# Two 16-head attentions and a rank-32 feed-forward in an eight-stage kernel: banks paired, set-up moved inside, small matmuls tiled

## What is computed

```python
# x: (32, 256, 128), 16 heads of 8 columns
x = x + _L0_attn_ref(_layernorm(x), Wq, bq, Wk, bk, Wv, bv, rel_bias)   # stage 1
#   scores = q.k / sqrt(8) + rel_bias[bucket(key - query)]; softmax; probs @ v
x = x + _L0_ffn_ref(_layernorm(x), w_up, w_down)                        # stage 2
#   _ternary_linear: alpha = mean(|w|); w_q = sign(w) * (|w| > 0.5 * alpha)
x = x + _L1_attn_ref(_layernorm(x), w_attn, b_attn, w_proj, b_proj)     # stage 3
#   causal attention, 16 heads, then y @ w_proj + b_proj
# stages 4 to 7: mixture of experts, state-space layer, routed experts, min-GRU
P = jnp.einsum('bsd,dr->bsr', x, U1)                                    # stage 8, r = 32
H = jax.nn.gelu(jnp.einsum('bsr,rf->bsf', P, V1) + b1)                  # f = 512
Q = jnp.einsum('bsf,fr->bsr', H, U2)
return jnp.einsum('bsr,rd->bsd', Q, V2) + b2
```

## Time and profile before

| | us |
|---|---|
| median of 3 runs (lowest, highest) | 4479.35 (4473.92, 4491.18) |
| the profiled execution, its own time | 4466.33 |
| its span, first to last instruction | 4464.5 |
| first attention, step b = 0 begins | 100.20 |
| first attention, step b = 28 begins | 726.04 |
| second attention, steps b = 1 and b = 27 begin | 1072.16, 1519.49 |
| last stage, first instruction | 4252.08 |

### The profile page before, as it was taken

The page is one execution under the profiler, slowest core; times in us unless marked ns, Lnnn a source line. Parts: engine busy times, 40 slices in busy tenths (PEclk is TensorE's granted clock), DMA queues, the critical chain, the costliest instruction groups (busy, mean ns, idle before and its releaser), DMA issues. The chain is left out here.

```text
span 4464.5 us, 64699 instructions
## 1 busy us (share of the span) xinstructions
PE 3708.3 (83%) x23220; PEld 2276.8 (51%) x23220; DVE 3003.3 (67%) x6733; ACT 1884.3 (42%) x3377; POOL 1552.6 (35%) x1036
## 2 busy tenths in 40 slices
PE   4999999787999962877478888888779999997589
PEld 2666666455777752544223333333346666664244
DVE  5788888555676736333279999999956566665922
ACT  1555554324666630222166666666522222222222
POOL 2111110352121101788477777777610100010300
PEclk9999999897999965899799999999989999998689
DMA  5333332004444430233322222222100000000000
GB/s 128 77 79 79 79 78 63 6 4 96 104 100 106 98 121 14 37 43 44 81 67 75 68 67 67 67 76 69 55 36 1 1 1 1 1 1 7 0 20 24
DMA packets 196385, 239.10 MB, mean 54 GB/s; under 512 B 35507, under 2 KB 148501, under 8 KB 185798
## 3 DMA queue, kind: packets, MB, share of 16 engines
q1 hardware_dynamic: 170502, 216.50, 18.5%
q0 software_dynamic: 22528, 17.32, 3.0%
q10 hardware_dynamic: 3040, 1.15, 0.1%
HBM read 178.21 MB, written 55.51 MB: 52 GB/s over the span
## 5 line engine op out<-in xcount | busy, mean ns | idle before, releaser
L418 DVE TENSOR_REDUCE a_Mx<-a_Sx 128x2 f32<-128x512 f32 (+1 forms) x1024 | 590.9, 617 | 200.1 <-PE a_Sx L477 120.1
L332 ACT ACTIVATE a_Pr<-a_Se 128x512 f32<-128x512 f32 (+1 forms) x1024 | 501.0, 541 | 494.3 <-DVE a_Se L425 330.0
L2018 POOL TENSOR_TENSOR a_inp<-a_dtu,a_Bs 128x1024 f32<-128x1024 f32 x256 | 604.7, 2383 | 94.6 <-DVE a_h L2182 93.4
L2182 DVE TENSOR_TENSOR_SCAN a_h<-a_dA,a_inp 128x1024 f32<-128x1024 f32 x256 | 584.1, 2282 | 5.1 <-POOL a_inp L2018 5.1
L2272 PE MATMUL a_Y<-a_hc,g_ident 128*128 128x512 f32 x1024 | 521.2, 634 | 2.5 <-DVE a_hc L2192 2.5
L277 POOL TENSOR_TENSOR a_rest<-a_qk,a_parts 128x512 f32<-128x512 f32 x64 | 74.0, 1157 | 999.1 <-ACT a_parts L308 999.1
L2110 ACT ACTIVATE a_dA<-a_dtA,a_A 128x512 f32<-128x512 f32 x512 | 331.4, 682 | 174.8 <-DVE a_h L2182 174.0
L474 PE MATMUL a_Sx<-a_Kp,a_Qp 96*128 96x256 bf16 (+1 forms) x2048 | 381.0, 263 | 20.6 <-DMA a_Kp<-a_packing 12.3
L1834 ACT ACTIVATE f_sg<-f_GB 128x512 f32<-128x512 f32 x272 | 162.4, 597 | 512.3 <-PE f_GB L1884 512.1
L1779 DVE TENSOR_TENSOR f_sg<-f_sg,f_UB 128x512 f32<-128x512 f32 x256 | 176.0, 687 | 282.7 <-PE f_CB L1891 255.8
L1917 PEld LDWEIGHTS f_OUT<-f_wd,f_hm 128*128 128x128 f32 x2176 | 287.0, 192 | 91.1 <-issue 82.0
(11 more groups left out here) (429 smaller groups left out, 7592.3 us busy)
## 6 DMA issues: line engine op xcount, KB each, us to landing
a_Bs<-a_brows SPq DMA_DIRECT2D x256, 256.0 KB, 3.3
a_Qp<-a_packing SPq DMA_DIRECT2D x192, 192.0 KB
a_Kp<-a_packing SPq DMA_DIRECT2D x192, 192.0 KB
a_packing<-a_parts SPq DMA_DIRECT2D x64, 384.0 KB
a_packing<-a_parts SPq DMA_DIRECT2D x64, 128.0 KB
g_x<-x SPq DMA_DIRECT2D x8, 512.0 KB, 7.4
f_sum<-g_x SPq DMA_DIRECT2D x1, 4096.0 KB, 13.1
f_w<-L_w SPq DMA_DIRECT2D x2, 2048.0 KB
```

Of the source, the lines that this page charges most:

```text
L332: nc.scalar.activation(Pr[h % NP][:, 0:K0Q + K1Q], Se[h % 2][:, 0:K0Q + K1Q], ACT.Exp).then_inc(s["exp_done"], 1)
L418: nc.vector.tensor_reduce(Mx[(k + 2 - (j < LATE)) % 2][:, t, 2 * jj:2 * jj + 2], Sx[t][:, 0:2 * wd].rearrange("p (h q) -> p h q", h=2), AX ...
L2018: nc.gpsimd.tensor_tensor(inp[n % Q][:], dtu[k][:], Bs[n % Q][:].unsqueeze(1).to_broadcast([P, CH, GT]), ALU.mult).then_inc(s["mulB"], 1)
L2182: nc.vector.tensor_tensor_scan(h[n % 2][:].rearrange("p c q -> p (c q)"), dA[m % 2][:].rearrange("p c q -> p (c q)"), inp[n % Q][:].rearra ...
```

## The change

- `load_x` is gone. The parts of `x` are fetched inside the first attention's block, the first part ahead of the weights; statistics and norm factors of the first eight tiles are made before step -3 and those of the other 56 tiles in VectorE's step b = -2. `BiasSetup.load` and the identities go to ScalarE's queue; its lines are copied by ScalarE. SyncE places the bias after the first batch's packing instead of before it; the bias of the farthest bucket is folded into constant rows (`CROW`), so that `bmax` has 160 columns a head.
- `Qp`, `Kp`, `V`, the ternary weights and the second attention's weights live in `attention_buffers`, held over stages 1 to 3; the second attention clears nothing, and its weights are fetched in step b = 4 of the first.
- `maxima`: the two heads' masks, or biases, are one matmul of 256 (or 320) columns. `scores` works on a pair of heads: bank `Se0` holds both heads' first 128 keys, `Se1` the others; the bias terms and masks of a pair are one matmul each, VectorE's addition and ScalarE's exponential cover a pair, and `scores` stands ahead of `maxima` in a sub-step.
- SyncE's packed reads of step b wait until the maxima rows of the same step have landed (`mpacked`).
- `quantize` is gone as a block: ScalarE makes the thresholds in steps -3 and -2, GpSimd applies them in step b = 4.
- `lowrank_ffn`: `U1` and `V2` are repeated four times instead of padded; `U` is four products with 32 contraction rows each, into four banks; `QQ` four products with 32-column weights, each into its own quarter of the partitions; `b2` is added to `x` by GpSimd; `qT` is double, the order is shifted by a group, and the weights are loaded in the stage before.

```diff
-        load_x(nc, res, a["x"])
-        for stage in STAGES:
-            stage(nc, res, a)
+        res["scope"] = sc
+        with ExitStack() as first:
+            res["held"] = attention_buffers(nc, first, a)
+            for stage in (l0_attn, l0_ffn, l1_attn):
+                stage(nc, res, a)
...
@@ attention, sync @@
+                def constants():
                     bias.place(sp)
                     sp.wait_ge(bias.crows_stored, NPART * 16)
+                    for k in range(BUF):
+                        sp.wait_ge(s["cleared"], k + 1)
+                        sp.wait_ge(s["k_cleared"], k + 1)
+                        sp.dma_start(Kp[k][MROW:MROW + 2], w["krows"][0:2]).then_inc(s["consts"], 16)
+                        sp.dma_start(Kp[k][CROW:CROW + 6], w["krows"][2:8]).then_inc(s["consts"], 16)
+                        sp.dma_start(Qp[k][CROW:CROW + 6], bias.crows).then_inc(s["consts"], 16)
+                    bias.place_band(sp)
...
                         wait(sp, s["written"], 32 * (b + 4))
+                        if m:
+                            wait(sp, s["mpacked"], 16 * (b + 2))
                         for j in range(3):
...
+                    if not causal and b == -3:
+                        constants()
+                    if not causal and b == 4:
+                        for n, t in held["second"].items():
+                            sp.dma_start(t[:], held["sources"][n]).then_inc(held["second_loaded"], 16)
@@ attention, gpsimd @@
+                    if not causal and b == 4:
+                        ternary()
@@ attention, scalar @@
+                        if c:
...
+                            nc.scalar.activation(probs[:, at:at + 2, 0:K0Q], pair(0, K0Q), ACT.Exp)\
+                                .then_inc(s["exp_done"], 1)
+                            wait(act, s["se_mm"], 16 * b + 2 * j + 2)
+                            nc.scalar.activation(probs[:, at:at + 2, K0Q:K0Q + K1Q], pair(1, K1Q), ACT.Exp)\
+                                .then_inc(s["exp_done"], 1)
@@ attention, vector @@
+                    if not causal and b == -2:
+                        n = 8
+                        for i in range(1, TILES // FIRST):
+                            n += part_stats(i)
+                        part_norm(FIRST, TILES, n, 2)
+                        clear_Q(2)
+                        clear_Q(3)
...
+                        if c and not causal:
+                            v.wait_ge(s["se_mm"], 16 * b + 2 * j + 1)
+                            near = pair(0, K0Q)[:, :, 0:BAND]
+                            nc.vector.tensor_tensor(near, near, band[:, 2 * j:2 * j + 2], ALU.add)\
+                                .then_inc(s["biased"], 1)
                         if (x_ if j >= LATE else m):
...
-                        if c and not causal:
-                            for h in (2 * j, 2 * j + 1):
...
@@ attention, tensor @@
-                            nc.tensor.matmul(Sx[t][:].rearrange("p (u q) -> p u q", u=2), flip[:],
-                                             bmax[:, 2 * j:2 * j + 2, P * (1 - t):P * (1 - t) + S],
-                                             start=True, stop=False)
...
+                            lo, hi = (0, P) if t == 0 else (FROM, S)
+                            last = nc.tensor.matmul(both[:, :, lo:hi], flip[:],
+                                                    bmax[:, 2 * j:2 * j + 2, P * (1 - t) + lo - FROM:P * (1 - t) + hi - FROM],
+                                                    start=False, stop=True)
...
+                            last = nc.tensor.matmul(both[:, :, wd - P:wd], identb[:],
+                                                    maskq[:].unsqueeze(1).to_broadcast([P, 2, P]), start=False, stop=True)
...
                         if b == -2 and j == LATE:
-
-                            pe.wait_ge(s["consts"], (BUF if causal else 2 * BUF) * 16)
+                            pe.wait_ge(s["consts"], (BUF if causal else 3 * BUF) * 16)
...
+                        if not causal and b == -1 and j == LATE:
+                            pe.wait_ge(s["thr_ready"], 2)
+                            pe.wait_ge(bias.band_placed, NPART * 16)
@@ ternary_ffn @@
-        wu, wd = sc.sb("wu", [P, C, P]), sc.sb("wd", [P, C, P])
-        quantize(nc, res, name, w, wu, wd)
+        wu, wd = res["held"]["wu"], res["held"]["wd"]
@@ lowrank_ffn, gpsimd @@
+                nc.gpsimd.tensor_tensor(xs, xs, b2[:].unsqueeze(1).to_broadcast([P, G, D]), ALU.add).then_inc(raised, 1)
@@ lowrank_ffn, tensor @@
                 if on(1):
+                    wait(pe, p_ready, g + 2)
+                    wait(pe, gelu, C * (g + 1))
+                    for c in range(C):
+                        r = slice(R * c, R * c + R)
+                        last = nc.tensor.matmul(U[c][:], v1[r, :], pT[r, :], start=True, stop=True)
+                    last.then_inc(up_mm, 1)
                 if on(0):
...
-                        last = nc.tensor.matmul(QQ[:], u2[:, c], hT[k][:, c], start=(c == 0), stop=(c == C - 1))
+                        last = nc.tensor.matmul(QQ[R * c:R * c + R, :], u2[:, c], hT[k][:, c], start=True, stop=True)
```

More of the change, by code:

```diff
@@ new lines, in maxima, with scores @@
+                        last.then_inc(s["mx_mm"], 1)
+                def scores(b, k, j):
+                    Q, K, h0 = Qp[k], Kp[k], 2 * j
+                    wait(pe, s["exp_done"], 16 * b + 2 * j - 1)
+                    for u in range(2):
+                        last = nc.tensor.matmul(pair(0, K0Q)[:, u], K[:, h0 + u, 0:P], Q[:, h0 + u, :],
+                                                start=(u == 0), stop=(u == 1 and not causal))
+                    if causal:
+                        last = nc.tensor.matmul(pair(0, K0Q)[:, :, 0:P], identb[:],
+                                                maskk[:].unsqueeze(1).to_broadcast([P, 2, P]), start=False, stop=True)
+                    last.then_inc(s["se_mm"], 1)
+                    wait(pe, s["exp_done"], 16 * b + 2 * j)
+                    for u in range(2):
+                        nc.tensor.matmul(pair(1, K1Q)[:, u], K[:, h0 + u, P:2 * P], Q[:, h0 + u, S - K1Q:S],
+                                         start=(u == 0), stop=False)
@@ L664, in look_up, with copy_lines @@
                 .then_inc(self.made, 1)
+    def copy_lines(self, act):
+        N, line = self.N, self.line
+        act.wait_ge(self.made, 3)
+        for i in range(3):
+            self.nc.scalar.activation(line[:, i * N:i * N + N], self.LP[i], ACT.Copy).then_inc(self.got, 1)
     def split(self, v):
```

563 lines of the change are left out of this document (294 added, 269 removed).

## The result

| | before | changed |
|---|---|---|
| median of four runs, us | 4480.02 | 4294.27 |
| lowest, highest | 4473.92, 4491.18 | 4291.76, 4296.79 |
| the profiled execution, its own time | 4466.33 | 4291.76 |

The ratio is 0.9587 with a 95% interval of 0.9553 to 0.9621: the changed kernel is 4.1% faster. The forecast was 4244 us with a range of 4185 to 4300. Direction and range held, the range by 6 us at its upper end, but the size was off by 50 us. That is the net of errors of opposite sign (two attentions 79 us too hopeful, the last stage 14.5 us too careful), so that the time stayed inside the range is partly luck. The total explains little; the stages do.

The account below looks back on a forecast made before the run. TensorE was taken as busiest in both attentions' full steps and the last stage, nothing as binding at the start. Savings of 22 + 69 + 6 + 12.6 + 20 + 105 = 235 us gave 4231, plus 13 for the median: 4244 us, range 4185 to 4300.

Parts of the forecast that it names:

- last stage: Low-rank stage: `QQ` and `U` products side by side cut a group from 12.0 to 5.5 us, saving 105 us.
- start: Before step 0: step 0 begins at 77.5 instead of 100.20, 22 us earlier; bounds 0 and 36.
- first attention, full steps: 28 steps of the first attention: 22.35 falls to 19.9 us each, stops on the maxima rows gone, saving 69 us.
- its run-out: End of the first attention, 82.60 us with about three steps of scores: 6 us saved.
- ternary stage: `quantize`: its loads move to the start's queue and its arithmetic under the first attention, saving 12.6 us.
- second attention: Second attention: fewer hand-offs save 9 us over 30 steps, the dropped clearing and loads 10.7; together 20 us.
- rival (c): Start: gains nothing, since the band's transfers delay the second batch until where it was; 4266 us, chance 0.10.
- Rival (a): First attention: pair hand-offs hold the step at 21.2 us and only the stops go; 4281 us, chance 0.17.
- rival (e): Both attentions: SyncE's wait on the maxima rows closes a ring, slower than before, 4659 us at c = 22; chance 0.03.
- Rival (d): Both attentions: narrow matmuls cost more than their columns, 1.6 us a step gained in the second; 4195 us, chance 0.10.
- Rival (b): Last stage: `U`'s row parts run one after the other, 42 us more; 4286 us, chance 0.08.

Follow-up runs that it names:

- e5: Changed kernel with `finish` late, the maxima's transposition and evacuation ahead of sub-step 5's scores and exponentials, and the second attention maxima first: 4202.12 us, ratio 0.9421.
- e3: Changed kernel with VectorE's `finish` in the first attention moved one sub-step later, behind the addition: 4257.25 us, ratio 0.9514.
- e1: Changed kernel with the order inside a sub-step turned back on all three engines, pairs and everything else kept: 4278.94 us, ratio 0.9559.
- e4: Kernel before with only the new order (scores, additions, exponentials first), single heads and unmerged masks: 4531.08 us, ratio 1.0123.
- e10: Kernel before with only `finish` moved behind the next sub-step's additions in the first attention: 4416.28 us, ratio 0.9877.
- e9: e1 (maxima first on all three engines) with `finish` of the first attention behind the next sub-step's addition: 4265.07 us, ratio 0.9539.
- e6: Changed kernel without SyncE's new wait on the maxima rows: 4336.65 us, ratio 0.9722.
- e12: e5 without SyncE's wait on the maxima rows: 4204.46 us, ratio 0.9401.
- e7: Changed kernel with TensorE adding `b2` again, by a one-row product behind each `v2` product: last stage 141.8 us against 92.9.
- e11: e7 with the product that adds `b2` given 128 rows, 127 of them zero: last stage 106.9 us.
- e8: Changed kernel with each `U` product padded with zeros to 128 rows, so the four cannot lie side by side: last stage 134.7 us.
- e2: Changed kernel with the order turned back on TensorE alone, maxima before scores: 4378.76 us, ratio 0.9788.

## Why the prediction was right or wrong

The terms are compared by landmarks in the two profiled executions (4466.33 and 4291.76 us).

| term | forecast | measured |
|---|---|---|
| start | 22 | 23.1 |
| first attention, full steps | 69 | 13.1 |
| its run-out | 6 | 2.9 |
| ternary stage | 12.6 | 13.4 |
| second attention | 20 | -3.0 |
| stages that no edit touches | 0 | 5.8 |
| last stage | 105 | 119.5 |
| sum | 235 | 174.8 |

**Ternary stage: right. Start: right in size, by another path.** Step 0 came at 77.1, forecast 77.5, and rival (c) is refuted. But the first maxima started at 52.8, not at 42.5, held by the constant rows of `Qp`, which landed later than I had them:

```profile
52.81 0.61 PE L617 MATMUL a_Sx<-att_Kp,att_Qp 96*128 96x256 bf16 x2 [26.05 <-DMA att_Qp<-a_crows]
```

After that TensorE never waited for the second batch's packed reads, on which my 77.5 rested. Two errors of ten microseconds cancelled, which is luck.

**First attention: the failed step.** It is the wait term of the step. The prediction put TensorE's own work at 19.2 us and let its scores "wait some 0.6 us" for the addition and the exponential of the pair before, which gave 19.9 (19.2 and 0.6 are 19.8). The step is 21.75. The work was sized well, since e5 reaches 19.71 with TensorE busy 155.38 of 157.67 us. The wait was taken as one late hand-off, while it is a closed ring of 5.48 us for two sub-steps through the exponential, the scores, the maxima, the reductions, `finish` and the next addition. e3 and e5 show its size: 21.8 to 20.57 to 19.71. One sentence led away from it: "I take 0.5, since scores ahead of `maxima` give ScalarE more time before the bank is wanted". I weighed the reordering only for the scores, as a gain, and never asked what now stands behind them. But turning the order back alone won next to nothing here (e1, 21.65), so it is not the order of scores and maxima alone that failed. VectorE's own work was 504.17 / 28 = 18.0 us a step, not the 17.5 of the prediction.

Rival (a), that the hand-off of pairs holds the step at 21.2 (4281 us), came closer than my forecast, and it was not all wrong. In each order that was run with both, the paired kernel's step is longer than the calm step with single heads, although TensorE has less to do in it:

| order | single heads | pairs |
|---|---|---|
| maxima first, `finish` early | 21.2 (before) | 21.65 (e1) |
| scores first, `finish` early | 21.28 (e4) | 21.75 (as changed) |
| maxima first, `finish` late | 21.03 (e10) | 21.82 (e9) |

I take this as a sign that pairs have a part in the ring, although their merged biases differ from the single heads' too. But e3 and e5 show that they do not hold the step up once `finish` and the transposition have moved. The stops did go, as predicted. Taking them at their mean of 1.15 us a step was right for the kernel before; in the new order without the wait they would have cost 46 us (e6). The ring that rival (e) was afraid of, through SyncE, does not show in e5: with the wait the kernel is as fast as without it (e12).

**Second attention: the gain from the order.** Here the reordering itself failed. The start gained about what was forecast. The steps got 0.5 us longer, not 0.3 shorter; e1 shows that the order did it (16.99 us, forecast 16.9). That the columns decide, not the number of matmuls, held: pairs of masks brought no more than the 0.2 us between 17.2 and 16.99. Rival (d), with 1.6 us a step in this stage, is refuted by that. The Trainium skill's figure for narrow matmuls in a row (TensorE: Matmul & The Clock Gate, "Back-to-back issue gap", about 81 ns at 128 columns) came near it, at 1.7 us a step by the prediction's estimate; neither e1 nor e5 shows such a gain.

**Last stage: right mechanism, one term too dear.** The sum had 5.5 us a group; the group takes 4.87. `U` 1.07 (forecast 1.0), `QQ` 1.00 (0.9) and `PP` 0.86 with 0.95 behind it (1.96) were right or close; `OUT` was 1.7 and takes 0.99. The rest of the miss, some 5 us, is in the ramp and the tail (92.9 - 15 x 4.87 = 20 us, forecast 25):

```profile
4219.14 1.14 PE L1118 MATMUL f_U<-f_pT,g_low_v 32*128 32x512 f32 x8 [0.35 <-DVE f_pT L1086]
4220.21 1.06 PE L1124 MATMUL f_QQ<-f_hT,g_low_u 128*32 128x512 f32 x8
4221.21 1.16 PE L1130 MATMUL f_OUT<-g_low_v,f_qT 128*128 128x128 f32 x8
4222.20 1.02 PE L1135 MATMUL f_PP<-f_xnT,g_low_u 128*128 128x512 f32 x2
```

I had taken the 0.42 us of the earlier trace rows as the price of a `v2` product. Half of it was its neighbour of one row (e7, e11). Rival (b), `U` in a row, is refuted by e8, which measures what the row parts save: 3.63 to 1.07 us, 3.4 times. The Trainium skill has 3.07 for this packing (same page, "Measured speedup vs the span model"); here it is slightly more.

**What stays open.** How much of the ring is due to pairs: no run has e5's order with single heads. The small difference between 21.65 and 21.82 in the order "maxima first" is not explained. What the lower clock costs in e7's ramp and tail was not separated. The 5.8 us of untouched stages lie within the 10 us by which these moved between executions.

## What to carry to other kernels

An edit that moves work ahead in one engine's queue moves something else behind a wait. Follow the ring from an operation back to itself through all queues, add it up, and compare it with the busiest engine's work, before giving the reordering any gain. An order is a property of several engines at once: turned back on TensorE alone it cost some 85 us (e2); turned back on all three it won 19 us in the second attention (e1). One that is the better in the first attention, which has a VectorE step between matmul and exponential, was the worse one in the second, which has none; that this step is the reason was not tested. A transfer that stalls an engine behind larger ones may need no new wait, only to be issued a microsecond earlier (e10, e12).

## What the hardware showed that I had not expected

- Float32 products of 128 columns on TensorE take 0.22 us from start to start among their like, and 0.42 when products of 128 rows and of one row alternate (e7 against e11, equal columns).
- A 16 KB transfer issued at least 0.2 us ahead of six reads of 192 KB never held TensorE up (e12), and issued no later than 0.12 us after the first of them it did so once in 30 steps (e10); issued 1.8 us after it in most steps, on another queue, it did so 23 times, by 2.2 us in the mean (e6).
- ScalarE was far from full in the second attention (276.96 of 507.98 us in e2), and still the place of two short evacuations in its queue changed the step from 19.5 to 17.0 us (e2, e1).
